# Three edits to the weight chain of a four-layer Trainium2 kernel: when two rounds of weights are fetched, and where half the rows are measured

## The reference, cut to what matters

```python
x = x + tanh(g_xattn[0]) * L0_xattn(layernorm(x), ctx, ...)
x = x + tanh(g_ffn[0])   * L0_ffn(layernorm(x), ...)      # 16 experts, best 6 of each row, and a shared one
x = x + tanh(g_xattn[1]) * L1_xattn(layernorm(x), ctx, ...)
x = x + tanh(g_ffn[1])   * L1_ffn(layernorm(x), ...)
...                                                       # layers 2 and 3
# L1_xattn, for 16 heads h with K = 128, D_CQ = 192, R = 64:
q_r = ((x @ Wq.T)[h] @ w_kc_q[h]) @ W_qr[h]
k_r = kv @ W_kr[h]
out = softmax(q_r @ k_r.T) @ kv @ w_kc_kv[h].T @ Wo.T
```

## Time and profile before

| what | value |
|---|---|
| median of 3 runs | 988.2 us (984.89, 988.2, 990.96) |
| the profiled execution | 998.41 us |
| its span, first to last instruction | 996.6 us |
| mean granted TensorE clock | 0.968 of full speed |
| busy: TensorE matmul / VectorE / ScalarE / GpSimd | 914.4 / 566.6 / 345.6 / 427.6 us |
| moved by DMA | 84.84 MB, mean 85 GB/s |
| chain stage, last expert matmul to first L95 | about 457.8 to 512.0 us |

### The profile page before, as it was taken

One profiled execution on the slowest core, in us unless ns is written; L12 is line 12 of the kernel. 1 busy time (PEld: TensorE's weight loads), 2 busy tenths in 40 slices (PEclk: granted clock), 3 DMA queues, 4 the chain that ended last, 5 costly groups with the idle time before them and its releaser, 6 DMA issues. The chain is left out here.

```text
span 996.6 us, 15037 instructions
## 1 busy us (share of the span) xinstructions
PE 914.4 (92%) x4939; PEld 687.3 (69%) x4954; DVE 566.6 (57%) x1061; ACT 345.6 (35%) x612; POOL 427.6 (43%) x337
## 2 busy tenths in 40 slices
PE   7999998988799999999959979898799797999997
PEld 4899996976566666667749957686478554566664
DVE  6788886659243434442478987677877441222221
ACT  3454543410133333433425436343154321112121
POOL 5787873030377887876422230630360015122223
PEclk9999999989899999998979999999999998999999
DMA  8321110049356436454520010100000394122211
GB/s 309 131 87 49 45 45 1 2 143 408 123 94 142 84 71 156 80 78 100 167 84 2 1 38 1 38 1 1 12 0 1 117 428 147 54 44 42 36 35 11
DMA packets 38595, 84.84 MB, mean 85 GB/s; under 512 B 9741, under 2 KB 27533, under 8 KB 36014
## 3 DMA queue, kind: packets, MB, share of 16 engines
q1 hardware_dynamic: 22062, 64.56, 18.4%
q0 software_dynamic: 16176, 19.31, 11.5%
q10 hardware_dynamic: 288, 0.07, 0.0%
HBM read 71.23 MB, written 20.68 MB: 92 GB/s over the span
## 5 line engine op out<-in xcount | busy, mean ns | idle before, releaser
L2569 PE MATMUL ffn_GU<-ffn_W,ffn_XTB 128*128 x252 | 91.4, 486 | 3.9 <-DVE ffn_XTB L2472 3.0
L1865 POOL DMA_INDIRECT out_x<-ffn_YB,ffn_XB x23 | 35.8, 1557 | 120.8 <-DVE ffn_YB L1993 118.4
L2044 PE MATMUL ffn_GU<-ffn_W,ffn_XTB 128*128 x184 | 85.0, 605 | 0.0
L2456 DVE TENSOR_TENSOR ffn_GB<-ffn_GU,ffn_BIAS 128x352 f32<-128x352 f32 x63 | 33.0, 524 | 90.7 <-PE ffn_GU L2569 72.6
L2274 POOL DMA_INDIRECT kept_MARKED<-scratch_rows,kept_IDX x63 | 62.2, 987 | 52.1 <-DMA scratch_rows<-ffn_WEIGHT 33.2
L2569 PEld LDWEIGHTS ffn_GU<-ffn_W,ffn_XTB 128*128 128x128 f32 x252 | 43.6, 191 | 37.1 <-issue 23.2
L2071 PE MATMUL ffn_DN<-ffn_W,ffn_HT 128*128 (+1 forms) x248 | 60.3, 387 | 7.1 <-ACT ffn_HT L1888 7.1
L2600 PE MATMUL ffn_DN<-ffn_W,ffn_HT 96*128 x252 | 64.8, 379 | 0.0
L1982 DVE COPY ffn_XTB<-ffn_XP 128x256 f32<-128x256 f32 x23 | 9.7, 424 | 86.3 <-PE ffn_XP L2053 86.3
L2044 PEld LDWEIGHTS ffn_GU<-ffn_W,ffn_XTB 128*128 128x128 f32 x184 | 33.1, 189 | 35.9 <-issue 33.4
L2071 PEld LDWEIGHTS ffn_DN<-ffn_W,ffn_HT 128*128 128x128 f32 x248 | 46.3, 195 | 16.2 <-ACT ffn_HT L1888 7.2
(11 more groups left out here) (528 smaller groups left out, 2487.7 us busy)
## 6 DMA issues: line engine op xcount, KB each, us to landing
ffn_W<-in_f_w SPq DMA_DIRECT2D x9, 1536.0 KB, 6.4
ffn_W<-in_f_w SPq DMA_DIRECT2D x16, 608.0 KB, 18.2
attn_W<-in_L_pairs SPq DMA_DIRECT2D x7, 1088.0 KB, 5.0
scratch_rows<-in_rows_empty SPq DMA_DIRECT2D x1, 2967.0 KB, 13.8
ffn_XB<-scratch_rows SPq DMA_DIRECT2D x23, 129.0 KB, 2.0
ffn_BIAS<-in_f_bias SPq DMA_DIRECT2D x1, 2816.0 KB, 15.4
kept_STAGE<-in_f_w SPq DMA_DIRECT2D x1, 2048.0 KB, 7.8
kept_NEXT<-in_L_pairs SPq DMA_DIRECT2D x2, 768.0 KB, 6.7
```

The costliest lines, as they stand in the source:

```text
L1865: pool.indirect_dma_start(out[:, :], bass.IndirectOffsetOnAxis(ap=XB[:, i % NB, D:D + 1].bitcast(I32), axis=0), YB[:, i % 3, :], None, bou ...
L2044: last = pe.matmul(GU[:, m, :], x, weights(e, k * 2 * HID3 + m * HID3, HID3), start=k == 0, stop=k == KD - 1)
L2456: dve.tensor_tensor(GB[:, n % 2, :], GU[:, n % 2, 0:2 * HID], BIAS[:, bass.ds(e * (2 * HID), 2 * HID)], ALU.add).then_inc(biased, 1)
L2569: last = pe.matmul(GU[:, n % 2, 0:2 * HID], XTB[:, i % 2, k * P:(k + 1) * P], flat[:, bass.ds(e * WIDTH0 + k * 2 * HID, 2 * HID)], start=k ...
```

## The change

Three edits, all within `latent_chain`.

1. SyncE: the weights of round 2 wait, ahead of their old waits, until scatter 59 has landed (TILES0 - 4 = 59, odd, so `sum_b`, count 16 x 30), which is the fifth of the eight. The weights of round 3 are issued after the four loads of the sums.
2. VectorE: in the last round tiles 0 to 3 are measured between the copy of A and the copy of BT, and half 0 is normalised between the copy of BT and the low part of Y. Tiles 4 to 7 are measured after that, then G's low parts 0 and 1, `normalise(1)`, and parts 2 and 3 as before. ScalarE's root for half 0 moves behind its copy of KR, the root for half 1 between the second and the third high part of G.
3. TensorE: the dummy matmuls after the chain go from 10 to 6.

```diff
--- before.py
+++ after.py
@@ -826,16 +826,20 @@
                 with nc.Block() as block:
                     @block.sync
                     def _(sp):
-                        for g in range(2, ROUNDS):
+                        def weights(g):
                             for c, rows, cols in SECTIONS:
                                 sp.wait_ge((kr_ps, bt_ps, y_ps)[c], g - 1)
                                 sp.dma_start(W2[g % 2][0:rows, :, cols], A["L1_pairs"][2 * g:2 * g + 2, 0:rows, cols].rearrange("a p n -> p a n")).then_inc(w_in[c][g % 2], 16)
+
+                        sp.wait_ge(sums_done[(TILES0 - 4) % 2], 16 * ((TILES0 - 4) // 2 + 1))
+                        weights(2)
                         for i in range(2):
                             sp.wait_ge(sums_done[i], 16 * ((TILES0 + 1 - i) // 2))
                         for half in range(2):
                             tiles = slice(T // 2 * half, T // 2 * (half + 1))
                             for dst, src in ((SUM, "sum_a"), (XN, "sum_b")):
                                 sp.dma_start(dst[:, tiles, :], DR[src].rearrange("(t p) d -> p t d", p=P)[:, tiles, :]).then_inc(taken[half], 16)
+                        weights(3)
 
                     @block.gpsimd
                     def _(pool):
@@ -857,14 +861,16 @@
                             if g > 0:
                                 act.wait_ge(g_ps, 4 * g)
                             act.activation(KR[:, :, :].rearrange("p a n -> p (a n)"), PB[:, 1, :], ACT.Copy).then_inc(kr_sb, 1)
+                            if g == ROUNDS - 1:
+                                early_root(act, measured, rooted)
                             act.wait_ge(y_ps, g + 1)
                             act.activation(y_part(g, 0), PB[:, 3, :], ACT.Copy).then_inc(y_hi, 1)
                             for h in range(4):
                                 act.wait_ge(g_ps, 4 * g + h + 1)
                                 act.activation(g_part(g, h, 0), g_bank(h), ACT.Copy).then_inc(g_hi, 1)
-                        early_root(act, measured, rooted)
-                        act.wait_ge(measured, T)
-                        nrm["deviation"](act)
+                                if g == ROUNDS - 1 and h == 1:
+                                    act.wait_ge(measured, T)
+                                    nrm["deviation"](act)
                         nrm["scalar"](act)
 
                     @block.vector
@@ -878,6 +884,11 @@
                                 dve.tensor_scalar(XN[:, t, :], X[:, t, :], MOM[:, t, 0:1], RSTD[:, t:t + 1],
                                                   ALU.subtract, ALU.mult).then_inc(nrm["xn_ready"], 1)
 
+                        def measure_half(h):
+                            dve.wait_ge(added, h + 1)
+                            for t in range(T // 2 * h, T // 2 * (h + 1)):
+                                measure(dve, stats, t).then_inc(measured, 1)
+
                         def g_low(g, h):
                             dve.wait_ge(g_hi, 4 * g + h + 1)
                             dve.tensor_tensor(g_part(g, h, 1), g_bank(h), g_part(g, h, 0).bitcast(F32), ALU.subtract).then_inc(g_lo, 1)
@@ -888,23 +899,22 @@
                             if g > 0:
                                 dve.wait_ge(bt_ps, g)
                             dve.tensor_copy(AF[:, :, :, 0:R], PB[:, 0, 0:4 * R].rearrange("p (a j r) -> p a j r", a=2, j=2)).then_inc(a_sb, 1)
+                            if g == ROUNDS - 1:
+                                measure_half(0)
                             dve.wait_ge(bt_ps, g + 1)
                             if g > 0:
                                 dve.wait_ge(g_ps, 4 * g)
                             dve.tensor_copy(BT[:, :, :].rearrange("p a n -> p (a n)"), PB[:, 2, :]).then_inc(bt_sb, 1)
+                            if g == ROUNDS - 1:
+                                normalise(0)
                             dve.wait_ge(y_hi, g + 1)
                             dve.tensor_tensor(y_part(g, 1), PB[:, 3, :], y_part(g, 0).bitcast(F32), ALU.subtract).then_inc(y_lo, 1)
                             if g < ROUNDS - 1:
                                 for h in range(4):
                                     g_low(g, h)
-                        for t in range(T):
-                            if t % (T // 2) == 0:
-                                dve.wait_ge(added, t // (T // 2) + 1)
-                            measure(dve, stats, t).then_inc(measured, 1)
-                            if t == T // 2:
-                                g_low(ROUNDS - 1, 0)
-                                g_low(ROUNDS - 1, 1)
-                        normalise(0)
+                        measure_half(1)
+                        g_low(ROUNDS - 1, 0)
+                        g_low(ROUNDS - 1, 1)
                         normalise(1)
                         g_low(ROUNDS - 1, 2)
                         g_low(ROUNDS - 1, 3)
@@ -965,7 +975,7 @@
                         for g in range(ROUNDS):
                             step(g)
                         pe.wait_ge(y_lo, ROUNDS)
-                        keep_busy(pe, PB[:, 3, :], 10)
+                        keep_busy(pe, PB[:, 3, :], 6)
                         nrm["tensor"](pe)
 
 
```

## The result

| | median (us) | runs |
|---|---|---|
| before | 989.5 | 984.89 to 990.96, 4 runs |
| after | 999.27 | 997.69 to 1001.36, 4 runs |

The ratio is 1.0108, 95% interval 1.0067 to 1.0149: slower by about 10 us, outside the range and on the side that had 0.04. A second pair gave 1.0106 (1.0054 to 1.0157).

The account below looks back on a forecast made before the run. It took the chain stage's scatter and sums chain as bound, with scatters held by weights. Sums 5.3 us earlier, mostly given back by round 3's late weights: stage end 510.7 for 511.76, so 988.2 - 1.1 = 987.1 us, range 979.5 to 992.0.

Parts of the forecast that it names:

- the side that had 0.04: Whole kernel: the outcome of a measurably slower time, given chance 0.04; same had 0.92, faster 0.04.
- the scatters: GpSimd's queue: scatters at issue pace until 59 lands at 469.7 us; 60 held by round 2's weights until 477.5.
- Ts: The time at which SyncE issues the sums: 486.87 us before, forecast 481.6, 5.3 us earlier.
- the queues take turns: Rival on the DMA engines: scatter 60 passes beside the weights, sums issued at 475.3, 7.9 us less, 980.3; chance 0.16.
- The straggler: Rival at scatter 60: last packets wait for the slowest DMA engine, sums at 484.1, 2.8 us more, 991.0; chance 0.27.
- part 2's cover: VectorE, round 3: the four moved measures, 2.2 us, are hidden beside TensorE's L944 and cost nothing.
- part 3: TensorE after the chain: six dummies instead of ten, 0.9 us less inside a wait, gain nothing.
- The tail behind Y's low part: VectorE at the stage end: measures, G low parts, normalise and turned rows take 8.8 us from 501.9, ending at 510.7.
- when round 3's weights land: SyncE's queue: first section lands 11.0 us after the sums are issued (10.2 to 12.5), so round 3 starts at 492.6.
- how long the clock stays down: TensorE, round 3: half clock for its first 3.6 us after 5.5 us of standing still.
- throughout, 1.4 later: TensorE, round 3: with half clock throughout, L944 would take 3.78 us and all would be 1.4 us later.
- All behind it is unchanged: After the chain stage: nothing changes, so the stage's 1.1 us gain carries to the kernel's time.

Follow-up runs that it names:

- wait for 59 only: The kernel before with one line more: round 2's weights wait for scatter 59, which puts both rounds of weights behind it; 992.2 us, 1.0038 of before.
- after, round 3's weights ahead of the sums: The changed kernel with round 3's weights moved ahead of the loads of the sums, right behind round 2's; 995.18 us, 1.0071 of before.
- ten dummies: The changed kernel with ten dummy matmuls after the chain again instead of six; 1009.34 us, 1.0098 of before.
- queue only: The kernel before with SyncE's edits alone; VectorE, ScalarE and the ten dummy matmuls as before; 1009.89 us, 1.0115 of before.
- weights of round 3 behind, only: The kernel before with only round 3's weights moved behind the loads of the sums, without the wait for scatter 59; 1001.36 us, 1.0135 of before.
- after again: The changed kernel, unchanged, measured a second time; 1008.56 us, 1.0106 of before.
- Clock kept in the gap: The changed kernel with 36 dummy matmuls on TensorE between rounds 2 and 3; 994.47 us, 1.0060 of before.
- clock kept throughout: The changed kernel with 36 dummies between rounds 2 and 3, 8 between the halves of the turned rows, 12 behind them; 1002.19 us, 1.0037 of before.
- order only: The kernel before with the new order on VectorE and ScalarE and six dummies alone, SyncE as before; 1000.66 us, 1.0032 of before.
- before with the clock kept: The kernel before with 46 instead of 10 dummies after the chain and 8 behind the turned rows; 996.14 us, 0.9972 of before.
- Split: The changed kernel without the wait for 59, only the first section of round 3's weights ahead of the sums, dummies in the gaps; 993.68 us, 0.9939 of before.

## Why the prediction was wrong

**Right in the number, partly by luck: the scatters.** They went at issue pace until 59 had landed, and the weights of round 2 went out at 14.1 us of the stage (forecast 469.7 - 457.8 = 11.9: 59 started 1.6 us later in the stage than counted, and landed 0.6 later). The sums went out at 23.2 and 24.9 for 23.8. But in the first run of after that isn't the forecast's way. It had scatter 60 held behind the load, 62 issued at 20 to 22 us of the stage and landed 1.2 us after its issue. The trace has the packets of 60 at 468.02 to 468.27 us, just ahead of the load's first packet at 468.40; 62 is issued at 16.7 us of the stage and lands some 5 us after its issue, because now its own packets are held: the 288 packets of 61 and 62 pass between 473.85 and 475.8 us. The two differences nearly cancel. In the second run of after 60 is held and 62 waits for it, as the prediction says, and Ts is 1.1 us later than forecast.

The step taken against "the queues take turns" was that the last scatters' packets pass only as SyncE's load runs out. With a load of 704 packets (192 + 256 + 256 runs of one row each) it comes out so. It isn't what holds them: in "wait for 59 only" and in "after, round 3's weights ahead of the sums" the load has 1408 packets, and the 288 begin after 497 and 458 of them, where they begin after 466 to 538 of 704 in five runs with the whole queue edit. That is 29 to 34 packets for each of the 16 DMA engines, some 5 us, whatever still follows. (In "ten dummies" scatter 60 got through after 166 packets and 61 after 497.) The Trainium skill ("DMA: Bandwidth & Descriptors", "Queues, rings and completion order") says that an engine serves its queue rows in turn, a packet at a time, and counts as a packet a group of typically 9 to 17 descriptors, at most 64. The profile's packets are single runs of a row. So the count of 1 beside 405 in the earlier trace rows, 25 an engine, doesn't speak against turns as such, as the prediction takes it to. Read as turns, the waits here are mostly two to three times as long as the typical size gives. What failed of that rival is its size: it let the packets of scatter 60 pass at once.

The straggler's bound was Ts = 482.7 - 457.8 = 24.9 us. The second run of after stands just there, with scatter 62's wait of 6.06 us; "queue only", "weights of round 3 behind, only" and "ten dummies" are 1.9 to 2.5 us below it and lose as much. So it isn't what decided.

**Right: part 2's cover, and part 3.** In after the measures of the first half cost TensorE nothing, because round 3 was later still (the copy of BT waited 2.95 us for TensorE alone). The cover is what makes it so: with SyncE as before, TensorE stands 5.08 us behind them. Beside late weights the new order does earn something: "queue only" ends its stage at 60.9, after at 57.8 and 58.9. The tail behind Y's low part took 511.13 - 502.74 = 8.4 us for 8.8.

**Wrong: when round 3's weights land.** The step put the first section at Ts + 11.0, at most + 12.5. Round 3 began at + 13.95, 13.1, 14.4 and 14.2 in after, after again, "queue only" and "ten dummies"; with dummies in the gap the section landed at + 13.1 and 12.7. Only in "weights of round 3 behind, only" it was + 11.6, within the forecast's bounds, and that run loses as much: that the section came later than forecast isn't by itself what made the loss. The sums' data were all but through as forecast, at Ts + 7.7 for + 8.0, though in after their last packets ended at + 9.9 and not, as before, at + 8.1. The mis-sized term is "2.4 us, and some 0.6 to land", which divided 0.69 MB by the rate of the whole load. A section has landed only when the slowest of the 16 DMA engines has its piece. In the trace of after the 16 landing marks of the first section, one of each DMA engine, run from 487.24 (Ts + 10.7, the forecast's value) to 490.44, and the quickest mark of the second section is at 489.43, a microsecond before the first section is complete. By then 1.6 of the 2.0 MB were in. Over all seven runs with these weights behind the sums the quickest engine is at Ts + 10.2 to 10.7, the slowest at + 11.6 to 14.4. Why the slowest lags more in some of them stays open. Behind the sums the section took 490.4 - 484.2 = 6.2 us instead of 3.0; round 2's took 5.6 us from issue with nothing of SyncE's ahead of it. The trace of before had such a number, in its list of DMA issues, which the prediction doesn't use:

```profile
kept_STAGE<-in_L_pairs SPq DMA_DIRECT2D x1, 672.0 KB, 5.2
```

That section went out alone, the next 3.7 us behind it, and it took 5.2 us for the same bytes, so a section needs that long without company too. With 5.2 the step would have given Ts + 8.0 + 5.2 = 13.2, where 11.6 to 14.4 were measured.

**Wrong: how long the clock stays down.** Forecast: round 3 at half clock for 3.6 us, from the earlier trace rows. Measured: until 499.3, 8.8 us into the round (8.5 to 10.9 in the four runs like it), and the round to the end of Y's matmuls (L952, in after L962) took 501.38 - 490.48 = 10.9 us where before took 6.7 and the forecast had 7.9. The 3.6 us came from a stretch in which dense transposes followed the idle time. Round 3's small matmuls are thin work, and round 0, in the same group, had shown 6.7 us for just that. That the thin work is the reason for the difference is argued from these two and wasn't tested. The bound "throughout, 1.4 later" ended at L944, whose 3.78 us are in the earlier trace rows. The price of a half-clock L928 was misread as well: the 2.44 us of the earlier trace rows run from 457.82 to 460.26, and the clock fell only at about 459.1. At half clock throughout it took 3.67. "Clock kept in the gap" shows the term by itself: 8.6 us for the round.

**Missing: the next stage.** From the end of L209 to the next stage takes 70.8 us in both runs of before and 73.1 and 73.2 in those of after. "All behind it is unchanged" was wrong, since the attention begins at the clock that the stage leaves: here L95 takes 0.76 us, with the clock kept throughout 0.47, and then the distance is 71.1. The same term makes "order only" and "wait for 59 only" slower (73.5 and 73.6 us), whose stages end hardly later than before.

By these terms, from the forecast stage end of 52.9 us: Ts -0.6, weights +2.95, clock +3.0, tail -0.4, together 57.85, measured 57.8. Then 2.3 for the attention.

**What stays open.** Both pairs of profiles place 7.5 us up to the next stage (131.5 against 123.95 in the mean). The medians differ by 10. The remaining 2.5 us lie behind it, where the code is the same and the time from there to the end differs by up to 10 us among all profiles (408.8 to 419.3). The three longest have 35 to 36 us at half clock there, the others 19 to 28. Whether the change moves those places or they move by themselves, one or two profiles a kernel can't tell: after has 28 and 35 us, before 24 and 19. The difference between after and before with the clock kept has the same gap: 6 us by the medians, 2.1 up to the next stage.

**Where the gain went.** The sums came 2.4 to 5.9 us earlier (23.2 and 24.9 against 29.1 and 27.3), and GpSimd's part was done early. But the rows wait for TensorE's chain too, and its slack was the 9.2 us of the earlier trace rows. The edit starts round 3 some 8 us later and adds 4.2 by the clock, and so turns the side chain into the end. Split keeps most of the slack, and there the early sums do count.

## What to carry to other kernels

When a load is moved behind another, take its landing from the list of issues, for the same section, and not from bytes over rate, and leave room for the slowest DMA engine: here it came 1.0 to 4.0 us after the quickest. Price idle time that you give to TensorE twice, once as itself and once as the clock for the work behind it, across the stage's end too. A wait that moves from one chain to another is a gain only up to the other chain's slack.

## What the runs showed of the hardware that was not expected

A round of small fp32 matmuls (52 of 64 to 256 columns) left the granted clock at 1.2 GHz for 8.8 us after work began again, where dense transposes had it back at 2.4 GHz in 3.6 us. The second isn't sure to happen: in "wait for 59 only" the same 3.68 us of transposes ended at half clock, and with the idle time behind them it was back only 6.1 us into the attention.

A small indirect DMA of GpSimd's behind a large load of SyncE's got through only after 29 to 34 of the load's packets on each DMA engine, about 5 us, with 704 as with 1408 packets in the load (seven runs; in an eighth, one scatter after 10).

Dummies alone, with no other edit, made the kernel before faster by 0.3%, just clear of noise: 0.9972 (0.9948 to 0.9996), with half clock in the stage and the attention down from between 10.2 and 17.1 us to 6.8. Its profile can't say where: its stage ends 0.8 to 2.3 us earlier, but its sums happen to go out 1.8 to 3.6 us earlier, which dummies behind the chain can't bring about.
